# Two gated cross-attention layers on one core: tail values as one set of 16 blocks, their adds on VectorE, and the masked layer's input norm on GpSimd

## What is computed

```
x = x + tanh(g_xattn[0]) * L0_xattn(layernorm(x), ctx)       # 16 heads of 32, 154 keys
x = x + tanh(g_ffn[0])   * L0_ffn(layernorm(x))              # 512 -> 2048 relu -> 512
x = x + tanh(g_xattn[1]) * L1_xattn(ctx, layernorm(x), mask) # norms of q, k, v per row of 512
x = x + tanh(g_ffn[1])   * L1_ffn(layernorm(x))              # gelu from a table, rounded to 1/256
# attention: q = x Wq; s = q k' / sqrt(32); p = softmax(s); y = (p v) Wo
```

## Time and profile before

| what | us |
|---|---|
| median of 3 runs (2407.03 to 2410.1) | 2409.3 |
| the profiled execution's own time | 2409.38 |
| its span, first to last instruction | 2407.6 |
| TensorE busy | 2352.2 (98%) |
| VectorE busy | 1504.9 (63%) |
| ScalarE busy | 1181.1 (49%) |
| GpSimd busy | 238.6 (10%) |

### The profile page before, as it was taken

One profiled execution on the slowest core, in us unless ns is written; L12 is line 12 of the kernel. 1 busy time (PEld: TensorE's weight loads), 2 busy tenths in 40 slices (PEclk: granted clock), 3 DMA queues, 4 the chain that ended last, 5 costly groups with the idle time before them and its releaser, 6 DMA issues.

```text
span 2407.6 us, 32695 instructions
## 1 busy us (share of the span) xinstructions
PE 2352.2 (98%) x12984; PEld 1793.4 (74%) x12984; DVE 1504.9 (63%) x2467; ACT 1181.1 (49%) x1912; POOL 238.6 (10%) x219
## 2 busy tenths in 40 slices
PE   7999999999999999999988999999999999999998
PEld 5566666688888888888765666666788888888886
DVE  5566666442222222223488888886988987988986
ACT  4554434442222222223335666666666666666665
POOL 1021112210000000000111111113000000000000
PEclk9999999999999999999998999999999999999999
DMA  3121112421101101102311111224301001110000
GB/s 130 36 88 53 53 54 80 161 80 53 50 4 53 53 1 53 53 3 86 121 64 50 67 68 67 67 71 145 105 29 43 36 36 36 36 38 33 36 35 19
DMA packets 89159, 140.95 MB, mean 59 GB/s; under 512 B 5040, under 2 KB 27952, under 8 KB 89008
## 3 DMA queue, kind: packets, MB, share of 16 engines
q1 hardware_dynamic: 89008, 138.87, 16.9%
HBM read 105.30 MB, written 33.55 MB: 58 GB/s over the span
## 4 chain that ended last, share of the span: by engine, by line
PE 39%; DVE 8%; ACT 2%; issue 2%; POOL 0%; DVEq 0%; ACTq 0%
PE l_lay_bank L69 19%; PE l_lay_score L69 11%; PE l_lay_score L1490 1%; PE l_lay_score L1546 1%; PE l_lay_score L1563 1%; DVE l_at_at_next L1089 1%; PE l_lay_score L1575 1%; PE l_lay_score L1567 1%; DVE l_at_h_lo L1103 1%; DVE l_at_at_next L1082 1%; PE l_lay_bank L1406 1%; DVE l_at_full L1078 1%; DVE l_at_full L1071 1%; DVE l_at_xTf_lo L975 1%; DVE l_at_maxes L1012 1%
## 5 line engine op out<-in xcount | busy, mean ns | idle before, releaser
L69 PE MATMUL l_lay_score<-l_at_tw_hi,l_at_h_hi 128*128 128x512 f32 x1024 | 401.5, 392 | 5.4 <-DVE l_at_h_lo L1103 4.8
L69 PE MATMUL l_lay_bank<-l_at_xTf_hi,l_at_tw_hi 128*128 128x512 f32 x1024 | 400.0, 391 | 0.0
L69 PE MATMUL l_lay_score<-l_at_tw_hi,l_at_h_lo 128*128 128x512 f32 x1024 | 398.8, 389 | 0.0
L69 PE MATMUL l_lay_bank<-l_at_xTf_hi,l_at_tw_lo 128*128 128x512 f32 x1024 | 398.4, 389 | 0.0
L69 PE MATMUL l_lay_bank<-l_at_xTf_lo,l_at_tw_hi 128*128 128x512 f32 x1024 | 398.4, 389 | 0.0
L69 PE MATMUL l_lay_score<-l_at_tw_lo,l_at_h_hi 128*128 128x512 f32 x1024 | 398.4, 389 | 0.0
L1063 DVE TENSOR_TENSOR l_at_h_lo<-l_at_full,l_at_h_hi 128x512 fp32r<-128x512 f32 x128 | 93.4, 729 | 468.5 <-ACT l_at_h_hi L760 468.5
L755 ACT ACTIVATE l_at_full<-l_lay_bank,l_at_lay_b 128x512 f32<-128x512 f32 x128 | 88.5, 691 | 456.6 <-PE l_lay_bank L69 456.6
L69 PEld LDWEIGHTS l_lay_score<-l_at_tw_hi,l_at_h_hi 128*128 128x128 f32 x1024 | 192.2, 188 | 49.3 <-DVE l_at_h_lo L1103 10.4
L69 PEld LDWEIGHTS l_lay_score<-l_at_tw_hi,l_at_h_lo 128*128 128x128 f32 x1024 | 192.2, 188 | 40.3
L69 PEld LDWEIGHTS l_lay_bank<-l_at_xTf_hi,l_at_tw_hi 128*128 128x128 f32 x1024 | 192.3, 188 | 40.1 <-issue 0.7
(11 more groups left out here) (196 smaller groups left out, 4063.0 us busy)
## 6 DMA issues: line engine op xcount, KB each, us to landing
both_x_in<-stream SPq DMA_DIRECT2D x25, 1024.0 KB, 5.6
l_at_xg<-stream SPq DMA_DIRECT2D x23, 1024.0 KB, 5.5
stream<-l_at_xg SPq DMA_DIRECT2D x22, 1024.0 KB, 4.3
l_at_tw_raw<-in_l_w SPq DMA_DIRECT2D x64, 256.0 KB, 5.5
both_x_in<-in_x SPq DMA_DIRECT2D x9, 1024.0 KB, 7.8
l_at_xg<-in_x SPq DMA_DIRECT2D x7, 1024.0 KB, 5.5
out<-l_at_xg SPq DMA_DIRECT2D x7, 1024.0 KB, 4.3
l_at_maskT_in<-in_maskT SPq DMA_DIRECT2D x16, 256.0 KB, 3.5
```

Of the source, the lines that this page charges most:

```text
L69: done = nc.tensor.matmul(out, lhs[a], rhs[b], start=first and n == 0, stop=last and n == len(passes) - 1)
```

## The change

The tail's values of all 16 heads are made by one function `tail_values`, right after the tail's exponentials, as 16 blocks of 32 x 32 that write `values` (t = 0) and `score[:, 1..3]`. Three copies take them to `c_sb` (t = 1 by VectorE; 2 and 3 by ScalarE), and for t = 1 to 3 VectorE adds the bank `values` to it (`c_add`) in place of ScalarE's copy. In the masked layer VectorE and ScalarE seed two banks each, GpSimd applies the input's norm (`norm_of`), `mask_front` and `maskT_front` stand earlier, and all four `q_low` stand between the maxima's rounds. Layer 0 also takes the third pair of banks. The projections on TensorE are put in other places.

```diff
+            def norm_of(it):
+                pool.wait_ge(x_rstd, it - made + 1)
+                for q in range(QT):
+                    nc.gpsimd.tensor_scalar(x_in[:, q, :], x_in[:, q, :], mv[:, q, 0:1],
+                                            rstd[:, q:q + 1], ALU.subtract, ALU.mult)\
+                        .then_inc(x_norm, 1)
...
                 if norm and it < last:
                     q_rstd_of(it + 1)
+                    norm_of(it + 2)
...
             def seed_main(it, t):
                 act.wait_ge(maskT_done, 2 * it + 2)
-                act.wait_ge(exp_done, NS * it + GH * t + GH)
-                nc.scalar.activation(score[:, GH - 1, :], mask_main[:, it % 2, :], ACT.Copy)\
-                    .then_inc(act_seeded, 1)
+                for j in (2, 3):
+                    act.wait_ge(exp_done, NS * it + GH * t + j + 1)
+                    if t == 0:
+                        act.wait_ge(tail_v_act, 2 * it + j - 1)
+                    nc.scalar.activation(score[:, j, :], mask_main[:, it % 2, :], ACT.Copy)\
+                        .then_inc(act_seeded, 1)
...
+            def c_add(it, t):
+                c = c_sb[:, it % 2, t, :]
...
+                dve.wait_ge(c_ps, KT * it + t + 1)
+                nc.vector.tensor_tensor(c, values, c, ALU.add).then_inc(c_out, 1)
...
                 if norm:
                     q_rows_front(it + 1, (0,))
+                    maskT_front(it + 1)
                     seed_main(it, 1)
                     q_rows_front(it + 1, (1,))
-                    mask_front(it + 1)
-                    maskT_front(it + 1)
                     if it:
                         c_mult(it - 1, (0, 1))
                     seed_main(it, 2)
...
                     seed_main(it, 3)
+                    c_add(it, 1)
                     q_norm_apply(it + 1)
                 else:
+                    tail_values_out(it, 1)
                     q_low(it + 1, (0, 1))
+                    if it:
+                        c_mult(it - 1, (0, 1))
                     norm_stats(it + 2)
-                    q_low(it + 1, (2, 3))
+                    q_low(it + 1, (2,))
                     norm_apply(it + 2)
...
-                        if norm and it >= 2:
+                        if it >= 2:
                             pe.wait_ge(c_normed, KT * (it - 2) + t - 1)
...
+                for t in range(KT):
+                    for j in range(GH):
+                        c = own_rows[group_of(t, j)]
+                        to = score[own_rows[j], t, :] if t else values[own_rows[j], :]
+                        done = nc.tensor.matmul(to, keys.v_tail[c, b, t, own_rows[j]], p_tail[c, t, :],
+                                                start=True, stop=t > 0, skip_group_check=True)
+                    if t:
+                        done.then_inc(tail_v_ps, 1)
...
-                for j in range(GH):
-                    own = slice(DH * j, DH * (j + 1))
-                    nc.tensor.matmul(values[own, :], keys.v_tail[:, b, t, own], p_tail[:, t, :],
-                                     start=True, stop=False, skip_group_check=True)
...
-                    q_front(it + 1, (0,))
+                    q_front(it + 1, (0,), (0, 1) if norm else range(KT))
                 else:
                     first_product(0)
+                tail_values(it)
+                if more and norm:
+                    q_front(it + 1, (0,), (2, 3))
+                    q_front(it + 1, (1,), (0, 1))
+                elif more:
+                    q_front(it + 1, (1,))
+                else:
+                    first_product(1)
                 scores_main(it, 0)
+                if it and not norm:
+                    recips(it - 1, (0, 1))
                 if more:
-                    q_front(it + 1, (1,))
+                    q_front(it + 1, (1,) if norm else (2,), (2, 3) if norm else range(KT))
+                if norm and it:
+                    recips(it - 1, (0,))
                 scores_main(it, 1)
```

More of the change, by code:

```diff
@@ L823, in _ @@
                 exps_tail(it)
-                if norm:
-                    seed_main(it, 0)
                 if it < B:
                     v_tail_of(it)
-                if not norm:
+                if norm:
+                    tail_values_out(it, 2)
+                    tail_values_out(it, 3)
+                    seed_main(it, 0)
+                else:
                     if more:
@@ L840, in _ @@
                         relu_hi(1)
+                exps_main(it, 0)
+                if norm:
+                    seed_main(it, 1)
+                if more and not norm:
+                    q_front(it + 1, (2,))
                 exps_main(it, 1)
@@ L966, in seed_main @@
                 dve.wait_ge(maskT_done, 2 * it + 2)
-                for j in range(GH - 1):
+                for j in range(2):
                     dve.wait_ge(exp_done, NS * it + GH * t + j + 1)
+                    if t == 0 and j == 1:
+                        if it < last:
+                            mask_front(it + 1)
+                        tail_values_out(it, 1)
+                        dve.wait_ge(tail_v_dve, it + 1)
                     nc.vector.tensor_copy(score[:, j, :], mask_main[:, it % 2, :]).then_inc(dve_seeded, 1)
@@ L1284, in _ @@
                     round_hidden(u)
-                else:
-                    relu_lo(u)
+            if not norm:
+                tail_values_out(last, 1)
+                relu_lo(0)
+                relu_lo(1)
+                c_add(last, 1)
             if norm:
@@ L1290, in _ @@
                 seed_main(last, 3)
+                c_add(last, 1)
                 c_low(last - 1, (0, 1))
                 c_mult(last - 1, (2, 3))
+                c_add(last, 2)
                 c_low(last - 1, (2, 3))
+                c_add(last, 3)
             else:
                 c_back(last - 1, (0, 1))
+                c_add(last, 2)
                 c_back(last - 1, (2, 3))
+                c_add(last, 3)
             y_back(last - 1, 0)
@@ L1443, in q_front @@
                         pe.wait_ge(q_row if norm else q_filled, KT * it + t - 1)
-                        if norm and it >= 2:
+                        if it >= 2:
                             pe.wait_ge(c_normed, KT * (it - 2) + t - 1)
-                    for k in range(KT):
+                    for k in ks:
                         if norm:
@@ L1607, in recips @@
                         pe.wait_ge(c_normed, KT * it + t - 1)
+                        if not norm and it + 2 < NCH:
+                            pe.wait_ge(q_filled, KT * (it + 2) + t + 1)
                     for q in range(QT):
@@ L1708, in _ @@
                     first_product(1)
+                scores_main(it, 0)
+                if it and not norm:
+                    recips(it - 1, (0, 1))
+                if more:
+                    q_front(it + 1, (1,) if norm else (2,), (2, 3) if norm else range(KT))
+                if norm and it:
+                    recips(it - 1, (0,))
                 scores_main(it, 1)
                 if norm and it:
-                    recips(it - 1, (0, 1))
+                    recips(it - 1, (1,))
                 values_of(it, 0)
-                if more:
+                if more and norm:
                     q_front(it + 1, (2, 3))
                 scores_main(it, 2)
-                values_of(it, 1)
+                if more and not norm:
+                    q_front(it + 1, (3,))
+                else:
+                    values_of(it, 1)
                 if norm and it:
@@ L1719, in _ @@
                 scores_main(it, 3)
-                if it and not norm:
-                    recips(it - 1, (0, 1))
+                if more and not norm:
+                    values_of(it, 1)
                 values_of(it, 2)
```

110 lines of the change are left out of this document (70 added, 40 removed).

## The result

The changed kernel takes 2434.6 us (median of 4 runs, 2432.6 to 2444.5) against 2409.7 for the kernel before (4 runs beside it). The ratio is 1.0117, with a 95% interval of 1.0103 to 1.0132: slower by 24.9 us. Its profiled execution took 2434.3 us. Forecast were 2452.3 us and a range of 2394 to 2482.

What follows compares the result with a forecast made beforehand. The prediction took TensorE, busy nearly throughout both layers' attention, as the bound: -39.2 us of tail work and new waits, largest +40.3, summed to +42.9 on 2409.4, so 2452.3 us, range 2394 to 2482.

Steps and rivals of the forecast that it cites:

- The tail's values, -2.45 us a chunk: Both layers, TensorE: tail values take 1.07 us a chunk instead of 3.52, -39.2 us over 8 chunks in 2 layers.
- The wait for `c_mult`: Layer 0: the third projection waits 2.55 us for `c_mult` 0 behind a held `q_low` 1, six chunks, +15.3 us.
- The smaller waits: Layer 0: `values_of` 2 waits 0.2 us for an add (+1.6), maxima round 4 0.7 us for the fourth `c_add` (+4.2).
- the first step of the prediction: TensorE bounds both attention layers; work removed is worth its length, and any new wait before it costs its whole length.
- the seeds, +1.2 and +0.4 us a chunk: Layer 1: `scores_main` 1 waits for ScalarE's second seed, +11.6 us in all; between blocks 2 and 3, +4.1.
- The masks, +8.2: Layer 1: `maskT_front` meets GpSimd's `add_bias`, so seeds behind it come 2.05 us late in four chunks.
- The waits of 3.5 us that were to go: Layer 1: TensorE's earlier wait for VectorE, where `add_bias` hit `mask_front` in full, would disappear: -3.5 us.
- The queries' norm, +40.3: Layer 1: GpSimd's norm holds VectorE's queries' norm one for one, delaying `values_of` 3 by 6.0 us in six chunks.
- the gap: The trace had no row of the float tensor_scalar of `q_norm_apply` beside a long GpSimd instruction.
- The last sign named: If the queries' norm stays near 2 us, the main step is wrong and the time is near rival 1.
- rival 1: The port is not held by these instruction pairs, so 56.3 us of terms fall away: 2396.0 us, faster; chance 0.18.
- Rival 2: VectorE keeps the port; only the first norm instruction delays it, 1.6 us in 7 chunks: 2423.2 us; chance 0.11.

Runs made afterwards that it cites:

- experiment 4: The changed kernel with layer 0's `c_mult` 0 and 1 put ahead of `q_low` 1 on VectorE: 2418.1 us, ratio 1.0036 to the kernel before.
- experiment 8: The changed kernel with GpSimd's `add_bias` issued as four instructions of 128x512 instead of one: 2411.6 us, ratio 1.0005 to the kernel before.
- Experiment 9: The four edits, with layer 1's blocks 1 to 3 seeded three by VectorE and one by ScalarE: 2388.5 us, ratio 0.9926.
- experiment 2: The changed kernel with layer 1's `maskT_front` moved behind the second query row: 2422.4 us, ratio 1.0054 to the kernel before.
- Experiment 1: The changed kernel with layer 1's input norm moved back from GpSimd to VectorE, behind `c_low` 0 and 1: 2444.1 us, ratio 1.015.
- Experiment 3: The changed kernel with GpSimd's norm tensor_scalar replaced by a tensor_tensor of the same shape, for timing only: 2461.2 us, ratio 1.0213.
- the four edits: The changed kernel with `c_mult` before `q_low` 1, `recips` 0 before `scores_main` 0, `maskT_front` after the second query row, `c_add` 2 before `c_low`: 2388.3 us.
- experiment 5: The changed kernel with layer 1's `c_add` 2 put ahead of `c_low` 0 and 1 on VectorE: 2423.1 us, ratio 1.0053.

## Why the prediction was right in its direction and too high

**The tail's values, -2.45 us a chunk: right.** 1.07 us in place of 3.52, in both layers.

**Layer 0, per chunk: right.** Forecast was -2.45 + 2.55 + 0.2 + 0.7 = +1.0. Clean chunks are +0.8 to +1.4 (51.8, 52.0, 52.4 against 51.0). The wait for `c_mult` sums to 15.4 us where 15.3 stood in the sum; that the two agree so well is in part chance, since five chunks wait 2.2 us on average, where 2.55 was forecast, and the first 4.5. Its cause, `q_low` 1 held by `add_bias`, was shown by experiments 4 and 8. The smaller waits were priced at 0.9 us a chunk and are 1.2 in a clean one. But layer 0 lost 10.1 us, not the 1.8 of the sum. The missing term is the **granted clock**: three of six chunks had stretches at TensorE's lower level (1.2 GHz instead of 2.4). TensorE is busy for 49.2 us in a clean chunk and for 51.7, 50.7 and 50.7 in these three (the first and third in the windows above): they cost 2.6 + 1.6 + 1.5 = 5.7 us. The rest of what the first is longer by is its longer wait, which the 15.4 hold already. Before, TensorE was busy without a break there and the clock stood at 1.00. With 2 us of waiting in each chunk it fell in some; with 0.5 (experiment 4) or 1.2 (experiment 8) in none of the six chunks. I had priced a wait at its own length, and the first step of the prediction said so; at 2 us and more a chunk it cost over a third as much again (5.7 on 15.4).

**Layer 1, the seeds, +1.2 and +0.4 us a chunk: right.** The block that waits for ScalarE's second seed, and its neighbours:

```profile
1550.19 0.60 PE L1685 MATMUL l_lay_bank<-ident,l_at_r_wide 128*128 128x128 f32 x4
1550.72 1.75 PE L1608 MATMUL l_lay_score<-l_at_qT_hi,l_at_k_hi 32*128 32x512 f32 x4
...
1553.10 0.66 PE L1685 MATMUL l_lay_bank<-ident,l_at_r_wide 128*128 128x128 f32 x4
```

`scores_main` 1 lasts from 1550.72 to 1553.10, 2.38 us against 1.13 unhindered: 1.25. Block 3 is 0.39 too long. These waits are in no row of waits, since the first matmul of the block starts in time and the later ones are late: the length of the group shows them. Experiment 9 adds that a third of a microsecond of it could be had, and not kept. One figure on the way there was off: by its own rows the block needs 1422.24 - 1418.19 + 0.49 = 4.54 us, not 4.35, and the term would be 1.4; 1.25 was measured.

**The masks, +8.2: right in kind, too small.** The hold is the 4.4 us of an instruction of 0.42 that takes 4.79, in three chunks. TensorE's wait is 2.89 instead of 2.05, and those three chunks are 3.8 to 4.9 us longer than the others, the fall of the clock behind the wait included: 12.5 us. Taking it away gave 12.2 (experiment 2). The waits of 3.5 us that were to go went.

**The queries' norm, +40.3: the step that failed.** As the prediction put it: "How two queues share is seen at 1424.96 [...] one of one, then one of the other, each held for the other's whole instruction. So the queries' norm takes four times 1.59 + 0.44". The rows were of other kinds of instruction. Beside GpSimd's tensor_scalar VectorE's norm takes 2.79 us against 1.92 (the first chunk, before GpSimd's first norm): 0.9 us in four instructions, not 6. The row of the first chunk:

```profile
1220.74 1.92 DVE L1026 TENSOR_SCALAR l_at_qn<-l_at_qn,l_at_lay_q_mv,l_at_lay_q_rstd 128x512 f32<-128x512 f32 x4
```

What stands in the term's place is 1.67 us a chunk of waiting for `c_add` 2, 10.7 in seven. The path was right, norm, products, low parts, add; its length was not. GpSimd's part in it can be read: 0.9 us in the norm and 0.4 in the two low parts (1.71 us against 1.28), 1.3 together. Experiment 1 fits: it takes these 1.3 us out of VectorE's queue and puts 1.9 in, and the wait grows by 0.5 us a chunk. Experiment 3 shows that the alternation exists: with a tensor_tensor on GpSimd in the same place VectorE's four take 5.32 us, and the kernel 26.6 us more. That rows of one kind do not price another was written down as the gap ("has no row of the former beside a long GpSimd instruction"), and given 0.18 and 0.11; it deserved more.

The rule of the Trainium skill on which that paragraph leaned (SBUF — State Buffer, Who interferes with whom: who issues first gets the pair for the whole instruction, the other fully blocks) agrees with `q_low`, with the mask and with experiment 3, and with the product from PSUM in experiment 4, which was free. It does not agree with GpSimd's tensor_scalar, beside which two of VectorE's four ran at their own pace, 0.54 us, while one GpSimd instruction was under way; the third, during which GpSimd went on to its next instruction, and the fourth took 0.94 and 0.98 us.

**The sum again.** With 10.7 for 40.3 the prediction's sum is +13.3; with the clock of layer 0 (5.7) and the masks (12.5 for 8.2) it is +23.3, and 24.9 were measured; by layers it is 7.5 for 10.1 in layer 0, of which the smaller waits explain 1.6 more, and 15.8 for 15.05 in layer 1.

Without the failed term the prediction's sum is +2.6 us, which is no change. So the direction that was forecast hung on this term, and that the kernel was slower all the same, by a wait a quarter as large at the same place and by a clock that no term held, was in part luck. The last sign named was wrong for the same reason: a queries' norm near 2 us does not bring the time near rival 1 (2396), but by the sum, with the other terms standing, to 2452.3 - 38.5 = 2413.8. Rival 2, 2423.2 us, named a price for the norm near the measured one (1.6 us in 7 chunks), but not its cause; rival 1's condition, under 13.4 of the 56.3 us left, was not met, since layer 0's and the mask's holds were real.

## What to carry to other kernels

A GpSimd tensor_tensor over 128 x 2048 in SBUF is a 4.6 us barrier for those VectorE instructions that read two SBUF tensors or convert a mask: split it, or put what TensorE waits for ahead of them, and try both alone, since they remove one cause. Where TensorE runs without a break, price a new wait of 2 us in each chunk at more than its length, because the granted clock can fall behind it: by over a third here. And before a term rests on a row, check that the row's pair of instructions is the pair in question; one kernel with that single instruction exchanged settles it.

## What the runs showed of the hardware

- GpSimd's tensor_scalar with two operands per partition takes 2.07 us for 128 x 512 f32 (28 of them, least 2067 ns), its tensor_tensor 1.27 to 1.48 us. The shorter one is the one that holds each of VectorE's instructions in turn.
- GpSimd pays too: beside the two `c_low` of VectorE, which read two SBUF tensors, its norm instruction took up to 2.58 us instead of 2.07, and one `c_low` 1.09 instead of 0.68.
- With the four edits all six chunks of layer 0 are between 49.48 and 49.57 us, at full clock; in the changed kernel the same work varied from 51.8 to 56.8.
- The clock in layer 0 as the changed kernel has it: five profiled executions ran that same code (the changed kernel and experiments 1, 2, 3 and 5). In each of them three chunks of six fell to 0.94 or 0.97, but not the same three. All nine chunks with a wait for `c_mult` of 2.8 us or more fell. Of the 21 with 2.0 to 2.6 us six fell. The first chunk always fell; there `q_low` 1 was held nearly for the whole of `add_bias`, 4.39 us.
- Open: which of the chunks with a short wait fall. One with 2.6 us stayed at full clock and one with 2.0 fell, in the same execution. No run here tells it.
